# Value projection with tokens on the output partitions: operand roles swapped, evacuation by ScalarE copies

## The reference, cut to what matters

```python
h = cond_ref(x, ...)                     # convolution over the 1024 features, masked
v = (h @ Wv.T).reshape(B, S, 8, 32)      # 2048 tokens x 1024 times 1024 x 256
out = einsum('bhqk,bhkd->bhqd', attn, v) # each value head serves 4 query heads
```

## Time and profile before

| | us |
|---|---|
| median of 3 runs | 945.55 |
| the profiled execution's own time | 945.55 |
| its span (first to last instruction) | 943.8 |
| TensorE busy | 898.5 (95%) |
| DVE / ACT / POOL busy | 449.5 / 208.9 / 396.5 |
| mean granted TensorE clock | 0.996 |

### The profile page before, as it was taken

How to read it: one execution, slowest core, us unless ns; L and a number is a source line. 1 busy time by engine, 2 the same in 40 slices (tenths; PEclk the granted TensorE clock), 3 DMA queues, 4 the chain that set the end, 5 groups by cost and what they waited for, 6 DMA issues and landing times.

```text
span 943.8 us, 23397 instructions
## 1 busy us (share of the span) xinstructions
PE 898.5 (95%) x10272; PEld 778.5 (82%) x10272; DVE 449.5 (48%) x935; ACT 208.9 (22%) x367; POOL 396.5 (42%) x296
## 2 busy tenths in 40 slices
PE   0899999999999999999799999999999999999997
PEld 0888989988888888887577777777789999999996
DVE  7556572111222222287877777788424333434334
ACT  4344642100000000051222222243222111101010
POOL 1244564303565567487777777777411000000000
PEclk9999999999999999999999999999999999999999
DMA  2679777211223222362543545442361122121211
GB/s 68 152 201 218 189 182 193 78 56 57 78 67 102 78 67 67 110 202 75 147 149 112 150 137 172 139 146 93 136 194 58 67 67 80 56 90 46 90 45 45
DMA packets 81925, 105.26 MB, mean 112 GB/s; under 512 B 41504, under 2 KB 54432, under 8 KB 81824
## 3 DMA queue, kind: packets, MB, share of 16 engines
q1 hardware_dynamic: 81312, 103.24, 37.6%
q0 software_dynamic: 512, 0.53, 0.2%
HBM read 74.08 MB, written 29.65 MB: 110 GB/s over the span
## 4 chain that ended last, share of the span: by engine, by line
PE 88%; DVE 3%; POOL 2%; issue 2%; DMA 2%; SPq 1%; ACT 0%; DVEq 0%; POOLq 0%
PE ps L807 20%; PE ps L1042 19%; PE ps L1254 19%; PE ps L525 9%; PE ps L769 5%; PE ps L536 4%; PE ps L1001 3%; PE ps L1222 3%; PE ps L981 3%; DMA toep<-kpad 1%; PE ps L1274 1%; PE ps L1275 1%; DMA wb_raw<-in_dram 1%; POOL rf L890 1%; PE ps L456 1%
## 5 line engine op out<-in xcount | busy, mean ns | idle before, releaser
L1254 PE MATMUL ps<-wb,xf 128*128 128x420 f32 (+1 forms) x1152 | 195.3, 329 | 1.9 <-DVE wb L1307 1.2
L1254 PEld LDWEIGHTS ps<-wb,xf 128*128 128x128 f32 x1152 | 189.3, 188 | 5.2 <-issue 2.6
L807 PE MATMUL ps<-y_hi,w_hi 128*128 128x512 f32 x320 | 125.2, 391 | 0.0
L807 PE MATMUL ps<-y_lo,w_hi 128*128 128x512 f32 x320 | 124.6, 389 | 0.0
L807 PE MATMUL ps<-y_hi,w_lo 128*128 128x512 f32 x320 | 124.6, 389 | 0.0
L525 PE MATMUL ps<-xc,toep 64*128 64x192 f32 (+4 forms) x1088 | 100.2, 336 | 11.4 <-DMA toep<-kpad 8.2
L525 PEld LDWEIGHTS ps<-xc,toep 64*128 64x128 f32 x1088 | 92.2, 191 | 15.4 <-issue 12.7
L1042 PE MATMUL ps<-y_hi,y_lo 128*128 128x512 f32 x256 | 103.8, 405 | 0.0
L1042 PE MATMUL ps<-y_hi 128*128 128x512 f32 x256 | 103.6, 405 | 0.0
L1042 PE MATMUL ps<-y_lo,y_hi 128*128 128x512 f32 x256 | 100.6, 393 | 0.0
L1087 POOL TENSOR_TENSOR sc<-sc,stat 128x1024 f32<-128x1024 f32 x32 | 61.9, 1936 | 52.2 <-DVE stat L1083 52.1
(11 more groups left out here) (147 smaller groups left out, 1321.8 us busy)
## 6 DMA issues: line engine op xcount, KB each, us to landing
toep<-kpad SPq DMA_DIRECT2D x64, 272.0 KB, 5.0
xc<-in_dram SPq DMA_DIRECT2D x32, 256.0 KB, 5.1
q_rows<-rf SPq DMA_DIRECT2D x32, 256.0 KB, 2.6
q<-q_rows SPq DMA_DIRECT2D x16, 512.0 KB, 4.8
xr<-in_dram SPq DMA_DIRECT2D x16, 512.0 KB
x_scratch<-xr SPq DMA_DIRECT2D x16, 512.0 KB, 3.2
x<-x_scratch SPq DMA_DIRECT2D x16, 512.0 KB, 3.6
out_dram<-x SPq DMA_DIRECT2D x15, 512.0 KB, 2.6
```

What stands on the lines that cost most here:

```text
L807: mm = pe.matmul(kq_bank(n), w[a][:, j, :], yt[b][:, j, g * 512:(g + 1) * 512], start=(j == 0 and a + b == 0), stop=(j == NJ - 1 and a == 1))
L1254: mm = pe.matmul(joint_bank(i, piece)[:, 0:hi - lo], xf[i % 2][:, a, t, :], wb[t][:, c, lo:hi], start=(t == 0 and a + c == 0), stop=(piece ...
```

## The change

The V projection swaps its operands. A block of 128 tokens of y is now the stationary operand, all 256 columns of Wv are the moving one. The output tile has 128 tokens on the partitions and 256 value channels; two such tiles fill a bank, 16 tiles fill 8 banks. The halves are gone, and the waits for all of `v_mask`, `a_yhi` and `g_ylo` stand before the first matmul. ACT empties the banks with plain copies (signal `a_v` for `v_v`), in place of DVE's transposes. `v_dram` is now token-major, 2048 rows of 256 numbers; each buffer is stored in two DMAs of 128 KB, and `stores_up_to` counts two for these. The loads of `vc` and the slices in `values` follow the new layout. The diff is whole:

```diff
--- before.py
+++ after.py
@@ -111,7 +111,7 @@
         kpad = nc.dram_tensor("kpad", [S, KROW + 1], F32, kind="Internal")
         k_dram = nc.dram_tensor("k_rows", [NG, P, TOK], F32, kind="Internal").ap()
         q_dram = nc.dram_tensor("q_rows", [NB, P, NQT, S], F32, kind="Internal").ap()
-        v_dram = nc.dram_tensor("v_rows", [NG, P, TOK], F32, kind="Internal").ap()
+        v_dram = nc.dram_tensor("v_rows", [TOK, NKV * HD], F32, kind="Internal").ap()
         x1_dram = nc.dram_tensor("x1_scratch", [TOK, L], F32, kind="Internal").ap()
 
         ps = ctx.enter_context(nc.psum_tensor("ps", [P, 8, 512], F32))
@@ -160,7 +160,7 @@
         q_0 = sb("q_0", [P, 2, NQT, S], F32, s2)
         kc = sb("kc", [P, 2, NG, P], F32, s2)
         VR = 4
-        vc = sb("vc", [P, VR, 4, 4, HD], F32, s2)
+        vc = sb("vc", [P, VR, 2, 2, 4 * HD], F32, s2)
         CR = 3
         sc = sb("sc", [P, CR, 1024], F32, s2)
         stat = sb("stat", [P, CR, 3, 16], F32, s2)
@@ -275,7 +275,7 @@
             "pe_conv", "v_mask", "a_yhi", "g_ylo")]
         a_whi, g_wlo, pe_unit = [signal(n) for n in (
             "a_whi", "g_wlo", "pe_unit")]
-        pe_v, v_v = signal("pe_v"), signal("v_v")
+        pe_v, a_v = signal("pe_v"), signal("a_v")
         pe_m, v_rot, v_rcos, g_rsin, g_rsum = [signal(n) for n in (
             "pe_m", "v_rot", "v_rcos", "g_rsin", "g_rsum")]
         g_zero3, a_w3, v_w3, g_w3 = [signal(n) for n in (
@@ -678,7 +678,7 @@
             gp.tensor_tensor(wsp[1][:, w_slot(m), :], wraw[:, w_slot(m), :],
                                         wsp[0][:, w_slot(m), :].bitcast(F32), ALU.subtract).then_inc(g_wlo, 1)
 
-        NVB = 4 * NG
+        NVB = TOK // P // 2
 
         Z = NU - 1
         TAIL = 4 * (NU - 3)
@@ -703,7 +703,7 @@
 
         def stores_up_to(n):
 
-            return 16 * (n // SR + 1)
+            return 16 * sum(2 if k < NVB else 1 for k in range(n % SR, n + 1, SR))
 
         def stored(eng, n):
             eng.wait_ge(st_stg[n % SR], stores_up_to(n))
@@ -712,9 +712,10 @@
             load_weights(sp, 1)
             load_weights(sp, 2)
             for n in range(NVB):
-                sp.wait_ge(v_v, n + 1)
-                g, h = n // NG, n % NG
-                sp.dma_start(v_dram[h, :, g * 512:(g + 1) * 512], rf[:, n % SR, :]).then_inc(st_stg[n % SR], 16)
+                sp.wait_ge(a_v, n + 1)
+                for t in range(2):
+                    tok = slice((2 * n + t) * P, (2 * n + t + 1) * P)
+                    sp.dma_start(v_dram[tok, :], rf[:, n % SR, t * 256:(t + 1) * 256]).then_inc(st_stg[n % SR], 16)
             for i, (m, g) in enumerate(ORDER):
                 n = NVB + i
                 if i % 4 == 0 and i // 4 + WR < NU:
@@ -757,33 +758,20 @@
         def qkv_matmuls(pe):
             yt = [p.rearrange("p j b s -> p j (b s)") for p in (y[0][:], y[1][:])]
             wv = [w[:, 0:2, :].rearrange("p a n -> p (a n)").rearrange("p (j d) -> p j d", j=NJ) for w in wsp]
+            pe.wait_ge(v_mask, S // 2)
             pe.wait_ge(v_ke, NHG)
+            pe.wait_ge(a_yhi, S // 2)
+            pe.wait_ge(g_ylo, S // 2)
             pe.wait_ge(a_whi, 1)
             pe.wait_ge(g_wlo, 1)
-
-            def value_tile(h, b0, b1, s0, s1):
-                out = ps[:, h, :].rearrange("p (b s) -> p b s", s=S)[:, 0:b1 - b0, s0:s1]
-                out = out if b0 == 0 else bank(h + NG * (b0 // 8))
-                for j in range(NJ):
-                    for a, b in PASSES:
-                        mm = pe.matmul(out, wv[a][:, j, h * P:(h + 1) * P], y[b][:, j, b0:b1, s0:s1],
-                                       start=(j == 0 and a + b == 0), stop=(j == NJ - 1 and a == 1))
-                return mm
-
-            pe.wait_ge(v_mask, S // 2 - 1)
-            pe.wait_ge(a_yhi, S // 4)
-            pe.wait_ge(g_ylo, S // 4)
-            for h in range(NG):
-                value_tile(h, 0, 8, 0, S // 2)
-            pe.wait_ge(v_mask, S // 2)
-            pe.wait_ge(a_yhi, S // 2)
-            pe.wait_ge(g_ylo, S // 2)
-            for h in range(NG):
-                value_tile(h, 0, 8, S // 2, S).then_inc(pe_v, 1)
-            for g in range(1, 4):
-                for h in range(NG):
-                    mm = value_tile(h, 8 * g, 8 * g + 8, 0, S)
-                    mm.then_inc(pe_v, 1) if (g, h) != (3, NG - 1) else mm.then_inc(pe_unit, 1)
+            for n in range(NVB):
+                for t in range(2):
+                    tok = slice((2 * n + t) * P, (2 * n + t + 1) * P)
+                    for j in range(NJ):
+                        for a, b in PASSES:
+                            mm = pe.matmul(ps[:, n, t * 256:(t + 1) * 256], yt[a][:, j, tok], wv[b][:, j, :],
+                                           start=(j == 0 and a + b == 0), stop=(j == NJ - 1 and a == 1))
+                mm.then_inc(pe_v, 1) if n < NVB - 1 else mm.then_inc(pe_unit, 1)
             for n, (m, g) in enumerate(ORDER):
                 if g == 0:
                     pe.wait_ge(a_whi, m + 2)
@@ -797,7 +785,7 @@
                     scores(pe, CR)
                 w = [x[:, w_slot(m).start, :].rearrange("p (j d) -> p j d", j=NJ) for x in wsp]
                 if m < 2:
-                    pe.wait_ge(v_v, 4 * m + g + 1)
+                    pe.wait_ge(a_v, 4 * m + g + 1)
                 elif n < TAIL:
                     pe.wait_ge(v_rcos, n - 7)
                 else:
@@ -820,6 +808,10 @@
 
         def qkv_hi(act):
             act.wait_ge(g_ylo, S // 2)
+            for n in range(NVB):
+                v_ready(act, n)
+                staging_free(act, n)
+                act.activation(rf[:, n % SR, :], bank(n), ACT.Copy).then_inc(a_v, 1)
             for n in range(4 * NU):
                 if next_weights(n) is not None:
                     weight_hi(act, next_weights(n))
@@ -835,10 +827,6 @@
             swap = [(i + HD // 2) % HD for i in range(HD)]
             v.wait_ge(g_ylo, S // 2)
             v.tensor_copy(causal[:], across(C("causal"), REP)).then_inc(v_causal, 1)
-            for n in range(NVB):
-                v_ready(v, n)
-                staging_free(v, n)
-                v.transpose(rf[:, n % SR, :], bank(n)).then_inc(v_v, 1)
             for n in range(4 * NU):
                 m, g = ORDER[n]
                 lead = n - LEAD
@@ -921,11 +909,11 @@
             if i >= VR:
                 sp.wait_ge(pe_o, 2 * (i - VR) + 2)
             sp.dma_start(kc[:, i % 2, :, :], k_dram[:, :, i * P:(i + 1) * P].rearrange("t p k -> p t k")).then_inc(ld_k[i % 2], 16)
+            rows = v_dram[i * P:(i + 1) * P, :].rearrange("(b j k) c -> k (b j) c", b=2, j=2)
             for quad in range(4):
                 G = quad // 2
-                keys = v_dram[G, :, i * P:(i + 1) * P].rearrange("(g k) c -> k g c", g=4)
-                sp.dma_start(vc[quad * HB:(quad + 1) * HB, i % VR, :, :, :].rearrange("p g a d -> p g (a d)"),
-                             keys).then_inc(ld_v[i % VR], 16)
+                sp.dma_start(vc[quad * HB:(quad + 1) * HB, i % VR, :, :, :].rearrange("p b j c -> p (b j) c"),
+                             rows[:, :, G * 4 * HD:(G + 1) * 4 * HD]).then_inc(ld_v[i % VR], 16)
 
         def load_q(sp, i):
             if i >= 2:
@@ -998,7 +986,7 @@
                         continue
                     rows = slice(quad * HB, (quad + 1) * HB)
                     for g in range(4):
-                        mm = pe.matmul(ps[g * HD:(g + 1) * HD, quad, 256:384], vc[rows, i % VR, g, 2 * b + j, :],
+                        mm = pe.matmul(ps[g * HD:(g + 1) * HD, quad, 256:384], vc[rows, i % VR, b, j, g * HD:(g + 1) * HD],
                                        probs[rows, g, :, j, :], start=(j == 0), stop=(j == late))
             mm.then_inc(pe_o, 1)
```

## The result

The changed kernel takes 954.28 us (median of four runs, 954.21 to 956.61) against 945.49 for the kernel before. The ratio is 1.0097, with a 95% interval of 1.008 to 1.0115: about 9 us slower. The forecast was 952.5 with a range up to 954.0; the direction was right, the time lies just above the range. The profiled execution, a fifth one, took 952.97 us with a span of 951.2, 7.4 more than before.

A forecast was written before the change was run, and what follows sets the result against it. TensorE, busy 95% of the span, was taken to bound the kernel and alone set the V stage's 44.37 us. 945.55 + 3.92 (late start) + 1.85 (more matmuls) + 1.2 (clock) gave 952.5 us, range 950.5 to 954.0.

The forecast's parts named there:

- Step 1, the early start goes: At the handover from convolution to V, TensorE waits for the last y_lo and starts later: +3.92 us.
- Step 2, more matmuls: In the V stage, 384 matmuls of 256 columns replace 96 of 256 and 144 of 512: +1.85 us.
- the rival on the other side: Not slower: contiguous columns let V's 256-column matmuls start faster than strided runs of 32, paying for the pause; chance 0.02.
- Step 3, the clock: After the new pause before V, TensorE's clock falls and its matmuls run slower for a while: +1.2 us.
- The upper bound of 2.9: Largest clock price after the pause, from the program's start: convolution instructions took 5.76 instead of 2.83 us after 8.2 idle.
- The rival in which the clock stays up: The clock doesn't fall after the pause before V, giving 951.3 us; chance 0.27.
- Steps 4 to 6: ACT copies for DVE transposes, smaller stores and changed V loads, value matmuls reading another place: 0 us each.
- equal gaps: Sign that everything after the V stage only lies 6 to 7 us later, with its gaps unchanged.
- The rival on a later shift: Something later moves: the clock fall at 455 vanishes or a gap before value matmuls shrinks; 949.5 to 951, chance 0.06.
- The text's margin for no measurable change: Staying within 0.2%, 1.9 us, of the old time would need the sum wrong by over 3.9 us; chance 0.03.
- a low clock at the price of 2.9: Rival: the low clock after the pause before V lasts as at the program's start, 954.2 us; chance 0.08.

The follow-up runs named there:

- experiment 1: Kernel before with only the late start: waits for all mask, y_hi and y_lo steps stand before the first V matmul; ratio 1.0068, median 950.07 against 944.94 us.
- experiment 8: Changed kernel with its V waits in the old order, v_ke, a_whi and g_wlo first; ran once, 955.21 us beside 948.40 of the kernel before.
- experiment 2: Kernel before with its six 512-column V tiles computed in halves of 256 columns, 384 matmuls in place of 240, early start kept; ratio 1.0029.
- experiment 10: Kernel before with 21 idle 512-column matmuls in TensorE's three idle places at the start of attention; ratio 1.0002.
- experiment 4: Kernel before with late start and 384 matmuls of 256 columns, operands not swapped, DVE transposes and old layout kept; ratio 1.0092, 953.73 us.
- experiment 7: Changed kernel with DVE instead of ACT emptying the banks by plain copies; ratio 1.0106 to the kernel before, median 951.63 us.
- experiment 6: Changed kernel with 12 idle 256-column matmuls between the waits for y_hi and y_lo; ratio 1.0077 to the kernel before, median 949.22 us.
- experiment 3: Changed kernel with 30 idle 256-column matmuls ahead of the three late waits, filling the pause; ratio 1.0071 to the kernel before, 951.06 us.

## Why the prediction was right in direction and short in size

*Step 1, the early start goes (+3.92).* Right. The tail of the convolution stands on the chain and TensorE waits for L636 for 4.03 us: 3.8 with the waits in the old order (experiments 1 and 8), 0.2 for the new order, which the forecast doesn't speak of: it counted one resume of 0.14 us, and in the diff a_whi and g_wlo are waited for last. Experiment 8 shows that part.

*Step 2, more matmuls (+1.85).* Right: +1.79 in experiment 2, 46.31 - 44.37 = +1.94 with the swapped operands at full clock. Contiguous columns are no faster than runs of 32 (0.1200 us each for the 288 contiguous ones of experiment 2, 0.1201 for the others in the earlier trace rows), so the rival on the other side had no ground.

*Step 3, the clock (+1.2).* This is the term that was mis-sized: 2.3 us in the profiled run. That the clock falls was right, in eight traces of eight. But the price was taken from the one fall at 455, of 3.4 us, where the work had resumed just ahead of it, less something for the part inside the pause. The pause here is longer, so the fall can come well ahead of the resume; then the low stretch doubled to 6.8 us, and the matmuls at half speed were 25 instead of about 15: 2.3 us in the profiled run. The upper bound of 2.9 came from a row with a longer pause, 8.2 us. For a pause of 4.0 the value belonged between the two rows, and the text put it below both. Nor is it shown that the clock was the cause in the second row; the profile reads 1.00 over those slow instructions:

```profile
28.00:30.00 2.00, 2.00 (x14) 1.86 (x12) 0.00 (x0) 0.00 (x0) 0.00 (x0) 1.00 1.01 229
```

And the 1.5 us of the fall at 455, though rightly added up as work, lay in a wait and not on the path there (experiment 10). In the V stage, where TensorE has no wait, the same low stretch costs its full price. The rival in which the clock stays up, to which 0.27 was given, never came.

*Steps 4 to 6 (0 each).* Right within what can be told. The copies, the stores and the K and Q stages with them: 234.8 us from the end of V to the score matmuls in both traces. The loads of V and the value matmuls: 7.1 us up to them in both. Experiments 4 and 7 agree, more coarsely.

*Behind the stage.* The forecast let nothing change there and named equal gaps as the sign of it. The gaps were not equal (1.13 and 2.80 us for 2.73 and 1.35), and the low clock at 471 cost 1.6 us that no step has. The rival on a later shift had this place but the other sign. In the profiled run the end of the program gave 1.8 back, by chance as far as is known.

*The sum.* 4.0 + 1.9 + 2.3 = 8.2 us with the long low stretch, 7.4 with the short one, against 8.8 between the medians. In the profiled run the convolution ended 0.6 us earlier than in the trace of before (175.58 against 176.2), which is why its span grew by 7.4 only: -0.7 + 4.0 + 4.3 in the stage, + 1.6 at 471, - 1.8 to the end. The 0.6 that is left of 8.8 was not traced to a place; it is under what the runs scatter, and less than what the low stretch at 471 costs in one run. With 2.3 for the clock and 0.2 for the waits the forecast would have read 953.8, near the measured 954.28. In the profiled run such a sum fits only because the 1.6 at 471 and the 1.8 to the end nearly cancel. The text's margin for no measurable change was off too: to stay within 1.9 us of 945.55 the sum of 952.5 would have to be wrong by 5.1 us, and 3.9 is the distance from 951.3. The range's upper end stood at 954.0 because a low clock at the price of 2.9 had a chance of 0.08; a long low stretch came in three of five traces of the changed kernel and its variants with the whole pause.

## What to carry to other kernels

An early start on the part of the data that is ready is worth more than the wait it hides: it also keeps TensorE's clock up, and of the 9 us lost here 4 are the wait and 1.3 to 2.4 the clock behind it. If such a start must go, some idle matmuls in the middle of the pause keep the clock up: the stage got 2.3 us shorter by them in the traces, though the times alone can't tell it. Price a fall of the clock from the row whose pause is most like yours, and where the low stretch may begin inside the pause, keep the double length in the range. Then ask what the next step waits for: a low stretch of 3.4 us cost 1.3 to 1.6 us where TensorE was the last to finish and nothing where DVE was. Two equal lengths of a long rest of the program prove little if other traces of it differ by 8 us; compare it piece by piece. Exchanging the operands so that the moving side has 256 columns instead of 512 costs about 13 ns for each added matmul, whatever its layout saves elsewhere on engines that were idle.

## What the runs showed of the hardware

- After a pause of 3.8 to 4.0 us the clock was at 1.2 GHz for 3.4 us (five traces) or for 6.8 (three); it could fall as late as 1.3 us after the work had resumed.
- With 1.66 us of matmuls between pauses of 2.0 and under 0.2 us it stayed at 2.4 GHz (experiment 6, one trace), and so it did with 3.85 us of them (experiment 3).
- Two semaphore waits, long fulfilled, behind the wait that ends last made the resume 0.35 us (four traces) instead of 0.14 (experiment 8).
- At 1.2 GHz 256-column matmuls start 0.213 us apart and at 2.4 GHz 0.120. The columns alone are 0.2133 and 0.1067 us, so nothing beyond them shows at the lower level and 13 ns do at the upper.
- The clock fell in attention too, at 455.5 in the kernel before, where TensorE had just resumed from a wait of 2.7 us; the 3.4 us at the lower level cost nothing there, as the next wait shrank from 2.8 to 1.35 us.
